# Layer 1's first batch on a Trainium2 core: another order of weight turns, scores and value passes

## The reference

```
a = layer_norm(context) * gamma + beta
Q = x1 @ Wq.T ; K = a @ Wk.T ; V = a @ Wv.T          # 16 heads of 32
scores = Q K^T * 32**-0.5, masked with -inf where the mask is false
out = softmax(scores) @ V, heads joined, @ Wo.T
result = x1 + tanh(gate) * out
```

## Time and profile before

| | us |
|---|---|
| median of 3 runs (2368.19 to 2369.85) | 2368.53 |
| the profiled execution | 2366.59 |
| its span, first to last instruction | 2364.8 |
| PE busy | 2325.2 (98%) |
| ACT busy | 1479.8 (63%) |
| DVE busy | 1160.8 (49%) |
| POOL busy | 297.9 (13%) |
| mean granted TensorE clock | 0.995 |

### The profile page before, as it was taken

How to read it: one execution, slowest core, us unless ns; L and a number is a source line. 1 busy time by engine, 2 the same in 40 slices (tenths; PEclk the granted TensorE clock), 3 DMA queues, 4 the chain that set the end, 5 groups by cost and what they waited for, 6 DMA issues and landing times. The chain is left out here.

```text
span 2364.8 us, 43939 instructions
## 1 busy us (share of the span) xinstructions
PE 2325.2 (98%) x14670; PEld 1898.9 (80%) x14670; DVE 1160.8 (49%) x2246; ACT 1479.8 (63%) x3458; POOL 297.9 (13%) x336
## 2 busy tenths in 40 slices
PE   7999999999999999999999999999999999999998
PEld 6877777777777777678888888888888888888886
DVE  7555555556665665633122122122156666666674
ACT  5777777787777777754222222222248778787876
POOL 1111100111111101310000000000231221212120
PEclk9999999999999999999999999999999999999999
DMA  7444444444444444532010011011144555545443
GB/s 199 103 118 116 116 107 105 106 107 107 106 107 107 116 116 99 159 117 76 20 53 36 18 53 38 16 53 41 49 149 128 146 133 148 137 140 146 137 127 90
DMA packets 148209, 239.11 MB, mean 101 GB/s; under 512 B 25616, under 2 KB 59696, under 8 KB 148160
## 3 DMA queue, kind: packets, MB, share of 16 engines
q1 hardware_dynamic: 146752, 238.05, 37.2%
q10 hardware_dynamic: 1408, 0.41, 0.1%
HBM read 86.28 MB, written 25.21 MB: 47 GB/s over the span
## 5 line engine op out<-in xcount | busy, mean ns | idle before, releaser
L794 ACT ACTIVATE score_ps<-score_ps,l_neg_max 128x512 f32<-128x512 f32 (+1 forms) x1024 | 568.5, 561 | 123.5 <-DVE l_neg_max L1050 121.4
L1050 DVE TENSOR_REDUCE l_neg_max<-score_ps 128x1 f32<-128x512 f32 (+1 forms) x768 | 496.1, 684 | 53.6 <-PE score_ps L1333 52.4
L1782 ACT ACTIVATE mlp_hidden<-score_ps,b_col 128x512 f32<-128x512 f32 x128 | 88.4, 691 | 503.4 <-PE score_ps L67 457.9
L1830 DVE TENSOR_TENSOR mlp_hidden_l<-mlp_hidden,mlp_hidden_h 128x512 fp32r<-128x512 f32 x128 | 92.2, 720 | 519.1 <-ACT mlp_hidden_h L1784 518.9
L65 PE MATMUL item_ps<-feats_h,weights_l 128*128 128x256 f32 (+1 forms) x1024 | 322.7, 315 | 3.9 <-DVE weights_l L973 3.1
L66 PE MATMUL item_ps<-feats_l,weights_h 128*128 128x256 f32 (+1 forms) x1024 | 319.1, 312 | 0.0
L814 ACT ACTIVATE l_probs<-score_ps 128x1024 f32<-128x1024 f32 x272 | 270.4, 1020 | 77.7 <-PE score_ps L1368 76.6
L67 PE MATMUL item_ps<-feats_h,weights_h 128*128 128x256 f32 (+1 forms) x1024 | 318.6, 311 | 0.0
L1333 PE MATMUL score_ps<-l_stack 97*128 97x512 f32 (+1 forms) x1024 | 300.6, 361 | 13.7 <-ACT score_ps L794 7.4
L1368 PEld LDWEIGHTS score_ps<-l_stack 99*128 99x128 f32 x1536 | 213.9, 192 | 48.1 <-issue 15.7
L1368 PE MATMUL score_ps<-l_stack 99*128 99x256 f32 x1536 | 244.6, 291 | 3.3 <-ACT score_ps L794 2.2
(11 more groups left out here) (166 smaller groups left out, 4173.7 us busy)
## 6 DMA issues: line engine op xcount, KB each, us to landing
l_stack<-room SPq DMA_DIRECT2D x256, 192.0 KB, 3.4
l_stack<-l_qk SPq DMA_DIRECT2D x254, 128.0 KB
l_stack<-room SPq DMA_DIRECT2D x128, 128.0 KB, 3.2
l_stack<-l_qk SPq DMA_DIRECT2D x254, 64.0 KB
l_tokens<-in_x SPq DMA_DIRECT2D x16, 512.0 KB, 3.4
l_tokens<-in_ctx SPq DMA_DIRECT2D x16, 512.0 KB, 4.3
l_stack<-room SPq DMA_DIRECT2D x128, 64.0 KB, 3.1
l_rows<-in_x SPq DMA_DIRECT2D x16, 512.0 KB, 4.1
```

The lines of the kernel that those rows point to most:

```text
L794: m = act.activation(e, e, ACT.Exp, bias=neg_max[:, q, h:h + 1], accum_out=row_sum[:, q, h:h + 1])
L1050: dve.tensor_reduce(out, bank, AXIS_X, ALU.max, negate=True).then_inc(max_done, 1)
L1782: act.activation(hidden[:, m % HBUF, :], hidden_ps[:, m % 4, :], ACT.Gelu_apprx_tanh, bias=b1_col[:, m:m + 1])
L1830: dve.tensor_tensor(hidden_p[1][:, m % HBUF, :], hidden[:, m % HBUF, :], f32(hidden_p[0][:, m % HBUF, :]), ALU.subtract).then_inc(hidden_l ...
```

## The change

Four things change, all in layer 1's first batch and the MLP's end.

- The stack of the first batch is signalled in parts: three for the first half (j = 0; 1; 2 and 3), two for the second. All its copies are issued by SP.
- The blocks of Wv are turned through the two banks `o_ps`, those of Wo through `item_ps`. So scores need not wait for the weights; turns wait for the low part of the turn two before, and the first two token turns of the next batch wait for the last two weight lows.
- Six score steps stand in `FIRST`, among turns and value passes; `iteration(1, 0)` has ten left. ACT and DVE follow the same new list.
- The MLP's end makes the key flags on 16 partitions (four small DVE operations), SP stores them to DRAM, and layer 1 loads them broadcast. SP's wait for layer 0's result moves to `iteration(1, 0)`, ahead of the first load that needs it.

```diff
-    STEPS_AT_FIRST = [4, 4, 4, 2, 2, 2, 2, 3, 3, 2] if first else [2, 2, 2, 2, 2, 2, 2, 2]
+    STEPS_AT_FIRST = [4, 4, 4, 2, 2, 2, 2, 3, 3, 2] if first else [0, 1, 1, 2, 2, 2, 1, 1]
-    FIRST_AHEAD = AHEAD if first else 0
-    PARTS_AT_FIRST = [...] if first else [[(0, 1, 2, 3)], [(0, 1, 2, 3)]]
+    FIRST_AHEAD = AHEAD if first else 6
+    PARTS_AT_FIRST = [...] if first else [[(0,), (1,), (2, 3)], [(0, 1), (2, 3)]]
...
-                    split_ops.append((u, score_ps[:, n % RING, :], [t[:, f, :] for t in w], scale))
+                    split_ops.append((u, (o_ps if w is wv else item_ps)[n % 2][:, :], [t[:, f, :] for t in w], scale))
...
-            FIRST = K_ITEMS + [("split", n) for n in range(2 * FB, SPLITS)]
+            TURNS = range(SPLITS_OF_Q, SPLITS)
+            SPLIT_OP, STEP = [("split", n) for n in range(SPLITS)], [("step", k) for k in range(FIRST_AHEAD)]
+            FIRST = (K_ITEMS[0:3] + SPLIT_OP[8:11] + STEP[0:1] + SPLIT_OP[11:12] + K_ITEMS[3:] + STEP[1:2] + SPLIT_OP[12:13]
+                     + STEP[2:3] + SPLIT_OP[13:14] + STEP[3:4] + SPLIT_OP[14:15] + STEP[4:6] + SPLIT_OP[15:])
...
-        FIRST_OF_ACT = [(), () if first else (HG - 1,)]
+        FIRST_OF_ACT = [(), ()]
...
-                sp.dma_start(mask_all, mask_src.partition_broadcast(P)).then_inc(any_loaded, 16)
-                sp.wait_ge(source_stored[0], source_stored[1])
+                sp.wait_ge(flags_stored, 16)
+                sp.dma_start(any_key[:, :], key_flags.partition_broadcast(P)).then_inc(any_loaded, 16)
...
+                if not first and isinstance(p, int) and p == 1:
+                    sp.wait_ge(source_stored[0], source_stored[1])
...
-                if n >= RING:
-                    pe.wait_ge(w_low, n - RING + 1)
+                if n >= TURNS[0] + 2 and not TURNS[FB] <= n < TURNS[FB] + 2:
+                    pe.wait_ge(w_low, n - 1)
+                if n in (TURNS[FB], TURNS[FB] + 1):
+                    pe.wait_ge(low_done, ITEMS - 1 + n % 2)
...
+                if not first and isinstance(b, int) and b == 1 and k < 2:
+                    pe.wait_ge(w_low, SPLITS - 1 + k)
...
-                    if not first and isinstance(a, int) and a == 0:
-                        pe.wait_ge(w_low, SPLITS)
...
+                pe.wait_ge(w_low, SPLITS_OF_Q)
+                for n in range(NT, ITEMS - 1):
+                    item(0, None, n)
+                turn_weights(TURNS[0])
+                turn_weights(TURNS[1])
+                quarters = itertools.count()
+                def between_last():
+                    q = next(quarters)
+                    if q == 1:
+                        turn_weights(TURNS[2])
+                    if q == 2:
+                        step_ahead()
+                    if q == 3:
+                        turn_weights(TURNS[3])
+                item(0, None, ITEMS - 1, between_last)
+                step_ahead()
+                turn_weights(TURNS[4])
+                step_ahead()
+                pe.wait_ge(w_low, SPLITS_OF_V)
+                v_share(0, 0)
+                turn_weights(TURNS[5])
+                step_ahead()
+                v_share(0, 1)
+                turn_weights(TURNS[6])
+                step_ahead()
+                step_ahead()
+                turn_weights(TURNS[7])
```

In the MLP, behind the mask of DVE (`m == 2` of the last chunk):

```diff
+                    dve.tensor_reduce(flags[:, 0:1], mask_raw[:, :], AXIS_X, ALU.max).then_inc(flags_step, 1)
+                    dve.wait_ge(flags_step, 1)
+                    dve.tensor_scalar(flags[:, 0:1], flags[:, 0:1], 0.0, None, ALU.is_gt).then_inc(flags_step, 1)
+                    dve.wait_ge(flags_step, 2)
+                    dve.reciprocal(flags[:, 1:2], flags[:, 0:1]).then_inc(flags_step, 1)
+                    dve.wait_ge(flags_step, 3)
+                    dve.tensor_tensor(flags[:, 2:3], flags[:, 0:1], flags[:, 1:2], ALU.mult).then_inc(flags_step, 1)
```

More of the change, by code:

```diff
@@ L144, with __init__ @@
     BANK = [0, 1, 2, 0, 1, 2, 3, 0]
-    def __init__(self, room, arena, feats, turn_ps, ident, vec, given, gate, mask, mask_rows):
-        self.gate, self.mask, self.mask_rows = gate, mask, mask_rows
+    def __init__(self, room, arena, feats, turn_ps, ident, vec, given, gate, mask, mask_rows, key_flags):
+        self.gate, self.mask, self.mask_rows, self.key_flags = gate, mask, mask_rows, key_flags
         self.room, self.arena, self.feats, self.turn_ps, self.ident = room, arena, feats, turn_ps, ident
@@ L218, in attention_layer @@
                     mask_rows, result, room, given, norm_room, ident, arena, feats, banks, vec=None,
-                    source_stored=None, load_ahead=None, ahead=None):
+                    source_stored=None, load_ahead=None, ahead=None, key_flags=None):
     first = layer == 0
@@ L265, in attention_layer @@
     AHEAD = RING
-    STEPS_AT_FIRST = [4, 4, 4, 2, 2, 2, 2, 3, 3, 2] if first else [2, 2, 2, 2, 2, 2, 2, 2]
+    STEPS_AT_FIRST = [4, 4, 4, 2, 2, 2, 2, 3, 3, 2] if first else [0, 1, 1, 2, 2, 2, 1, 1]
     STEPS_IN_SLOT = [3, 5, 5, 1, 1, 1, 1, 4, 4, 3] if first else [1, 1, 1, 1, 0, 3, 3, 2]
     AFTER_T = SLOT.index(("item", NT))
-    FIRST_AHEAD = AHEAD if first else 0
-    PARTS_AT_FIRST = [[(0,), (1,), (2, 3)], [(0, 1), (2, 3)]] if first else [[(0, 1, 2, 3)], [(0, 1, 2, 3)]]
+    FIRST_AHEAD = AHEAD if first else 6
+    PARTS_AT_FIRST = [[(0,), (1,), (2, 3)], [(0, 1), (2, 3)]] if first else [[(0,), (1,), (2, 3)], [(0, 1), (2, 3)]]
     V_AHEAD = 1 if first else 2
@@ L342, in attention_layer @@
             tanh_gate = vec["tanh_gate"]
-            any_key, any_inv, gate_b = (sb(n, [P, B]) for n in ("any_key", "any_inv", "gate_b"))
-            mask_all = probs[PROBS - 1].bitcast(mybir.dt.uint8).rearrange("p (b s) -> p b s", b=B)
+            any_key, gate_b = (sb(n, [P, B]) for n in ("any_key", "gate_b"))
         item_ps, score_ps, o_ps = banks
@@ L351, in attention_layer @@
         raw_loaded = [sem(f"raw_loaded{n}") for n in range(2)]
-        q_loaded, o_loaded = sem("q_loaded"), [sem(f"o_loaded{n}") for n in range(2)]
-        late_vec_loaded = sem("late_vec_loaded")
+        if first:
+            q_loaded, o_loaded = sem("q_loaded"), [sem(f"o_loaded{n}") for n in range(2)]
+            late_vec_loaded = sem("late_vec_loaded")
         w_turned, w_high, w_low = sem("w_turned"), sem("w_high"), sem("w_low")
@@ L357, in attention_layer @@
         setup_step = sem("setup_step")
+        flags_stored = None if first else sem("flags_stored")
         tokens_loaded, item_done, high_done, low_done, part_done = (
@@ L430, in attention_layer @@
             SPLITS_OF_V = 3 * FB
-            FIRST = K_ITEMS + [("split", n) for n in range(2 * FB, SPLITS)]
+            TURNS = range(SPLITS_OF_Q, SPLITS)
+            SPLIT_OP, STEP = [("split", n) for n in range(SPLITS)], [("step", k) for k in range(FIRST_AHEAD)]
+            FIRST = (K_ITEMS[0:3] + SPLIT_OP[8:11] + STEP[0:1] + SPLIT_OP[11:12] + K_ITEMS[3:] + STEP[1:2] + SPLIT_OP[12:13]
+                     + STEP[2:3] + SPLIT_OP[13:14] + STEP[3:4] + SPLIT_OP[14:15] + STEP[4:6] + SPLIT_OP[15:])
+            assert SPLITS_OF_Q == 8 and SPLITS == 16
         def raw_view(u):
@@ L941, in _ @@
                     split_high(n)
[L942 to L945, removed]
                 else:
@@ L980, in vectors_ready @@
                     return
+                dve.wait_ge(any_loaded, 16)
+                dve.wait_ge(setup_step, 1)
+                dve.tensor_scalar(gate_b[:, :], any_key[:, :], tanh_gate[:, 0:1], None, ALU.mult).then_inc(part_done, 1)
                 dve.wait_ge(part_done, 1)
[L983 to L998, removed]
             def layer_norm_stats(b):
@@ L1138, in iteration @@
                         copy_v(a, SLOT[slot][1])
[L1139 to L1142, removed]
+                    if not first and isinstance(a, int) and a == 0 and slot == SLOTS:
+                        vectors_ready()
                 norm_next = not first and p is not None and not (isinstance(p, int) and p == B - 1)
@@ L1493, in iteration @@
                         item(p, a, n, step)
-                    if a is not None and SLOT[slot][0] == "share":
+                    if a is not None and SLOT[slot][0] == "share" and (first or not (isinstance(a, int) and a == 0)):
                         v_share(a, 0)
@@ L1531, in iteration, with step_ahead @@
                 project(a, 3)
[L1533 to L1544, removed]
+            ahead_steps = iter(range(FIRST_AHEAD))
+            def step_ahead():
+                scores(stack_of(0), 0, next(ahead_steps))
+            if first:
+                for n in range(ITEMS - 1):
+                    item(0, None, n)
+                item(0, None, ITEMS - 1, step_ahead)
+                pe.wait_ge(w_low, SPLITS_OF_V)
+            else:
+                pe.wait_ge(w_low, SPLITS_OF_Q)
+                for n in range(NT, ITEMS - 1):
+                    item(0, None, n)
+                turn_weights(TURNS[0])
[13 more added lines that the diff above has]
```

(17 more changed lines are left out.)

## The result

| | before | changed |
|---|---|---|
| median, first set (8 runs each) | 2369.36 us | 2376.51 us |
| median, second set (19 and 8 runs) | 2369.81 | 2376.15 |
| ratio, first set, 95% interval | | 1.0030 [1.0020, 1.0039] |
| ratio, second set | | 1.0029 [1.0019, 1.0040] |
| span of the profiled execution | 2364.8 | 2375.0 |

The changed kernel is 0.3% slower: +7.2 us (2376.51 - 2369.36), +6.3 in the second set. The forecast was 2375.1, that is +6.6 on the 2368.53 of the three earlier runs.

A forecast was written before the change was run, and what follows sets the result against it. PE, busy 98% of the span, was taken as the bound. Holes from the new order (+4.9 us) and a clock fall (+1.7) summed to +6.6 on the 2368.5 median, giving 2375.1 us; range 2368.5 to 2378.

The forecast's parts named there:

- The chain: Layer 1's first batch: DVE maxima and weight lows, ACT sums and highs never overlap; 2.84 us per link.
- Who waits: PE holes at the last weight turn and first two token turns, waiting for weight lows: 1.6, 2.4 and 3.1 us.
- The sum without the clock: Loss from the new order up to the next batch's fourth item, at full clock: +4.9 us.
- The last sign: Next batch's fourth item would start at 1776.5 to 1779.5 in place of 1771.69.
- The clock: PE's clock falls to half between 65 and 69 (us after 1700), released 2 to 5 us into full work: +1.7 us.
- Score 12: Next batch: it waits for sum 8, behind the last token turn's high on ACT; hole 1.3 us.
- Flags, parts, queues: Key flags cost 0; signalling in parts works; SP's issue of the second half is covered by 4 us.
- the rival of late parts: Stack copies contend, score 0 and the chain slip 1 to 3 us: +8 to +9.6, 2377 to 2378; chance 0.04.
- The chain without a fall: Rival: the holes in layer 1's first batch come but the clock stays full: +4.9, 2373.4; chance 0.16.
- The overlap: Rival: ACT and DVE overlap, 1.4 us per link, low 15 comes 4.3 us earlier: +0.6, 2369.1; chance 0.10.
- The ceiling of 4.7 us: Most that any repair of PE's holes at layer 1's start could gain: 4.7 us, 0.2% of the time.

The follow-up runs named there:

- b1: Changed kernel with maxima ahead of weight lows, last two splits ahead of sums 4 and 5, and ten score steps laid out anew; 2367.22 us, ratio 0.9994.
- a1: Changed kernel with only DVE's queue reordered, maxima 2, 3 and 4 each one place earlier, ahead of a weight low; 2371.61 us, ratio 1.0008.
- b3: As b1, but the ten steps laid out as 2, 0, 0, 0, 2, 2, 2, 2, two scores ahead of the token turns; 2367.97 us, ratio 0.9996.
- b5: As b1, but four scores in place of six among the turns, the other twelve laid out as 2, 0, 2, 0, 2, 2, 2, 2; 2367.22 us, ratio 0.9991.

## Why the prediction was right

Times of the changed kernel are given less 3.13 us, the later start of layer 1 in its profile.

- *The chain.* Forecast 2.84 us per link, measured 2.86. That the order on the two queues makes it: shown. DVE's order alone takes 3.9 us back, and b1, with the banks, flags, parts and PE's order in front of the token turns as in the changed kernel, is at 40.07 in place of 47.73.
- *Who waits.* The first token turn was put at 66.4 and came at 66.40 (1769.53), the second at 70.1 and came at 70.13 (1773.26); their holes are 2.2 and 2.5 by the view, which counts from the modelled end, some 0.16 less than the forecast's count. The second was put at 3.1; it is shorter because the turn and the score ahead of it ran in part at half clock (0.85 and 0.78 us). The last weight turn was put at 63.5 and came at 63.59, with a hole of 1.76 for the 1.6 forecast.
- *The sum without the clock.* Forecast +4.9, measured +4.9 with the holes filled. There score 12 comes at 76.76 (1778.47 less 1.71, the later start of that profile), where the forecast had 76.7.
- *The last sign.* The fourth item of the next batch was put between 1776.5 and 1779.5; it starts at 1781.76, which is 1778.63 on the scale of before.
- *The clock.* Forecast a fall between 65 and 69 for +1.7. It fell at 66.7, for 6.8 us, and cost 1.5. Two profiles of the changed kernel show the same measure to 0.01 us. That it would fall was argued from the earlier trace rows; how long it would last has no such row. The forecast's release, 2 to 5 us into the full work, is shown by no row of before; it came 3.3 us in. A fall of 10.2 us as in the earlier trace rows would have ended at 76.9, 6.8 us into the full work, for about 3.4 us (an estimate). So the size of this term was in part luck. The Trainium skill (TensorE: Matmul & The Clock Gate, section "HAM oscillation — how this bites in real kernels") warns of waits between short bursts; the trace agrees with it here, at 0.89 us busy of 4.80 ahead of the fall. In the Trainium skill's own case (same section) each wait is one for a DMA, of about 3 to 5 us; those ahead of the fall here were 1.8 and 2.2, so that case alone would not have decided between +4.9 and +6.6.
- *Score 12.* Forecast a hole of 1.3 by ACT's order behind the last token turn: the view shows 1.12 at 1781.42. It names a token low of DVE there, but the score's wait is for sum 8: that sum starts at 1780.35, and 1.07 later, as forecast, is 1781.42. Its maximum is of 1777.80; the sum stood behind the high of 1779.86.
- *Flags, parts, queues.* The flags cost 0.0, as forecast. The parts by themselves give -0.7 (-0.6 was expected ahead of that run). SP issued the second half from 59.8 (1762.90) to 70.0, as forecast, and PE shows no wait for a stack DMA in the changed kernel, so the rival of late parts is out. What ACT's four copies would have cost in the chain was not tested.
- *Rivals.* The chain without a fall (+4.9) is what the run with the holes filled shows, and not the changed kernel. The overlap that would have ended at +0.6 needs another order, and exists: with the order of b1 the same instructions come to -1.2. The ceiling of 4.7 us was not reached by any order tried; the best takes 1.6.

What was less exact: the sum on the median was +6.6, the medians give +7.2 and +6.3, and the measure +6.5. The median of 2376.51 is 1.4 above the forecast's 2375.1, 0.8 of it because the median before came out at 2369.36 in place of 2368.53. The rest is within what layer 1's start scatters. Where my later expectations failed (a1, b1, b3), it was by a queue order or a clock fall that I had not followed far enough.

## What to carry to other kernels

When two engines hand work to each other in both directions (max to sum, high to low), write both in-order queues side by side and look for a cycle: an item that stands behind one that waits for the other engine's previous item. Put each hand-over one place ahead of what it doesn't need, and the same instructions overlap. Work that is "free" in the bound engine's holes is not free if it lengthens a chain that this engine waits for; and several such holes in a row can cost once more through the clock, here 1.5 us on top of 4.9.

## What the runs showed that I had not expected

The clock also falls at the seam of layer 0 and the MLP, whatever is changed in layer 1, and not for the same length in every execution. In the profile before it was 10.2 us; in the second profile of the changed kernel 17.1:

```profile
994.10:1011.20 17.10, 15.73 (x69) 9.60 (x70) 12.26 (x24) 13.02 (x29) 7.84 (x8) 0.50 0.48 127
```

A shorter fall lies between 30 and 70 us in nine of the eleven profiles taken. Added up over pieces of 10 us to 1740, the clock is at half for 10.2 us in the profile of b1, whose layer 1 starts first (1740.1), and for 23.8 us in the second profile of the changed kernel, whose layer 1 starts last (1746.9). The MLP between takes 692.9 to 693.0 us in all eleven, and what stands behind the measure 581.9 to 583.0. So the scatter arises ahead of the MLP, and it goes with the clock, but not to the last us: the profiles of b5 and of the parts alone both have 17.0 us at half clock and start layer 1 at 1743.9 and 1742.2. What else moves it stays open.

These 6.8 us are more than the effect of any order here, and about as much as the timed runs of the kernel before scatter (2366 to 2372). The measure, taken inside the profile, repeated to 0.01 us in the one pair of profiles of the same kernel.

Transposes held the clock: with 48 transposes of the identity in the holes it stayed at 1.00 over the stretch in which it falls without them. The Trainium skill (TensorE: Matmul & The Clock Gate, section "Part 4: PE-mode transpose") says that the full clock does not engage for transposes, since they don't count as busy in the same way. Here they kept a clock that was already full; whether they would bring it up from half is not shown.
